# Convolution products as strips of the array: blocks 2 to 5 in four strips of 32 columns, blocks 6 to 8 in two of 64

## The reference

```
x = x + displaced(group_norm(x), offset)     # 48 groups of 8 channels
x = x + hadamard(group_norm(x))              # along the channels, 384 of 512
```

## Time and profile before

| | |
|---|---|
| time, median of 2 runs | 352.71 us |
| span of the profiled execution, first to last instruction | 361.2 us |
| PE / PEld busy | 162.4 us (45%) / 98.4 us (27%) |
| DVE busy | 246.9 us (68%) |
| ACT busy | 159.2 us (44%) |
| POOL busy | 124.9 us (35%) |
| convolution products L595, whole run | 306 matmuls, 41.3 us; 306 weight loads, 40.7 us |

### The profile page before, as it was taken

How to read it: one execution, slowest core, us unless ns; L and a number is a source line. 1 busy time by engine, 2 the same in 40 slices (tenths; PEclk the granted TensorE clock), 3 DMA queues, 4 the chain that set the end, 5 groups by cost and what they waited for, 6 DMA issues and landing times.

```text
span 361.2 us, 3084 instructions
## 1 busy us (share of the span) xinstructions
PE 162.4 (45%) x804; PEld 98.4 (27%) x804; DVE 246.9 (68%) x322; ACT 159.2 (44%) x205; POOL 124.9 (35%) x62
## 2 busy tenths in 40 slices
PE   0000004682796890300000008677676776767782
PEld 0000003682796790300000003222222222222230
DVE  1999999771874764100000047999999999899995
ACT  1029994940311200100000078787777777687720
POOL 0000000000521112000000007797979797979750
PEclk9999999995698996555555558698989889898898
DMA  6999999994388974373373300724996566874449
GB/s 227 414 410 409 409 370 355 406 249 102 71 216 216 279 210 122 53 87 44 44 87 44 44 0 17 292 100 186 356 373 248 191 147 198 311 294 181 190 181 360
DMA packets 21545, 76.67 MB, mean 212 GB/s; under 512 B 3824, under 2 KB 3952, under 8 KB 21376
## 3 DMA queue, kind: packets, MB, share of 16 engines
q1 hardware_dynamic: 18992, 69.62, 57.0%
q0 software_dynamic: 1616, 4.78, 4.8%
q10 hardware_dynamic: 912, 2.02, 4.7%
HBM read 46.42 MB, written 29.99 MB: 212 GB/s over the span
## 4 chain that ended last, share of the span: by engine, by line
DMA 25%; DVE 18%; issue 18%; another core or an unknown queue 16%; SPq 9%; ACTq 5%; ACT 5%; PE 2%; DVEq 0%; POOLq 0%
DMA ring<-x_pad 19%; DVE ring L917 9%; DVE parts L260 6%; SPq L267 5%; ACTq L267 5%; ACT blk L513 3%; DMA ring<-x_rows 2%; DMA blk<-x_pad 2%; DMA stat_rows<-blk_stat 2%; ACT parts L546 1%; SPq L271 1%; PE ps L656 1%; DVE blk_half L845 1%; PE ps L573 1%
## 5 line engine op out<-in xcount | busy, mean ns | idle before, releaser
L656 PE MATMUL ps<-parts,had_sb 128*128 128x512 f16 x384 | 101.6, 426 | 101.9 <-DVE parts L260 98.3
L513 ACT ACTIVATE blk<-ring,gn 128x1024 f32<-128x1024 f32 x48 | 58.6, 1230 | 85.4 <-DMA ring<-x_rows 59.9
L656 PEld LDWEIGHTS ps<-parts,had_sb 128*128 128x128 f16 x384 | 39.5, 107 | 163.7 <-DVE parts L260 105.2
L260 DVE TENSOR_TENSOR parts<-blk,parts 128x1024 f16<-128x1024 f32 x33 | 64.1, 1948 | 2.5 <-ACT parts L546 2.5
L917 DVE SCALAR_TENSOR_TENSOR ring<-ps,ring 128x1024 f32<-128x1024 f32 x48 | 57.2, 1210 | 0.0
L249 POOL TENSOR_TENSOR other_a<-blk 128x1024 f32<-128x1024 f32 x8 | 24.2, 3025 | 90.8 <-ACT parts L546 73.4
L253 POOL TENSOR_TENSOR blk<-blk 128x1024 f32<-128x1024 f32 x15 | 48.4, 3224 | 1.2
L582 PE MATMUL ps<-geo_sb,blk 128*128 128x128 f32 x72 | 13.6, 357 | 69.6 <-DMA blk<-x_pad 56.3
L595 PE MATMUL ps<-parts 128*128 128x64 f32 (+4 forms) x306 | 41.3, 301 | 7.3 <-ACT parts L475 6.2
L546 ACT ACTIVATE parts<-blk 128x1024 f16<-128x1024 f32 x40 | 41.2, 1048 | 4.2 <-POOL blk L253 2.8
L595 PEld LDWEIGHTS ps<-parts 128*128 128x128 f32 x306 | 40.7, 216 | 8.1 <-ACT parts L475 6.6
(11 more groups left out here) (105 smaller groups left out, 116.0 us busy)
## 6 DMA issues: line engine op xcount, KB each, us to landing
ring<-x_pad SPq DMA_DIRECT2D x20, 1536.0 KB, 15.3
out<-ring SPq DMA_DIRECT2D x13, 1536.0 KB, 6.3
blk<-x_pad SPq DMA_DIRECT2D x18, 512.0 KB, 8.3
x_rows<-blk POOLq DMA_DIRECT2D x9, 512.0 KB, 4.3
out<-ring SPq DMA_DIRECT2D x9, 512.0 KB, 3.7
ring<-x_rows ACTq DMA_DIRECT2D x5, 384.0 KB
ring<-x_rows SPq DMA_DIRECT2D x4, 384.0 KB
ring<-x_rows SPq DMA_DIRECT2D x9, 128.0 KB
```

The lines of the kernel that those rows point to most:

```text
L260: eng.tensor_tensor(parts[:, n % 2, 1, s, :], source, parts[:, n % 2, 0, s, :], ALU.subtract).then_inc(low_done[s], 1)
L513: act.activation(target, ring[:, t, place_of(i), :], ACT.Identity, bias=gn[:, t, i % BATCH, 1:2], scale=gn[:, t, i % BATCH, 0:1]).then_inc ...
L656: last = pe.matmul(sums[:, h, :], had_sb[:, sign, :], parts[:, n % 2, part, s, 512 * h:512 * (h + 1)], start=(at == 0 and part == 0), stop ...
```

## The change

One table `STRIP` gives each fast block a width, 128, 32 or 64. Where the width is below 128, each of the 17 products of the block is issued once for every strip: the stationary operand is cut along its columns (the pictures), and the result along the partitions of PSUM. The moving operand is the same for every strip. Blocks 0 and 1 keep one product of 128 columns.

```diff
+STRIP = (128, 128, 32, 32, 32, 32, 64, 64, 64)
...
-            def convolve_block(sums, pixels, weights):
+            def convolve_block(sums, pixels, weights, strip=128):
...
-                                last = pe.matmul(sums[:, bank, 32 * (a - 16 * bank):32 * (b - 16 * bank)],
-                                                 pixels[:, j, :], weights[:, a - (4 * j - 1):b - (4 * j - 1), :],
-                                                 start=(j == 3 * bank), stop=(j == 3 * bank + 4 and b == hi))
+                                for c in range(0, 128, strip):
+                                    last = pe.matmul(sums[c:c + strip, bank, 32 * (a - 16 * bank):32 * (b - 16 * bank)],
+                                                     pixels[:, j, c:c + strip], weights[:, a - (4 * j - 1):b - (4 * j - 1), :],
+                                                     start=(j == 3 * bank), stop=(j == 3 * bank + 4 and b == hi))
...
-                convolve_block(ps[2 + k % 2], flip[:, k % 2], conv_w[:, k]).then_inc(convolved, 1)
+                convolve_block(ps[2 + k % 2], flip[:, k % 2], conv_w[:, k], STRIP[k]).then_inc(convolved, 1)
```

## The result

The changed kernel took 359.67 us (358.97 to 360.37, 2 runs) against 352.71 us: a ratio of 1.0198, interval 1.0108 to 1.0287. That is inside the predicted range, at the edge of "within 2%". The first thing the profiles say, however, is that TensorE did not cost it.

What follows compares the result with a forecast made beforehand. ACT's walk over the row table, then nine patch transfers, was taken to bound the kernel, not PE. 14.4 us added to PE less 11 us covered gave 3.4 us, so 352.7 became 356 us; range 351.5 to 374.

Steps and rivals of the forecast that it cites:

- The gate: Before the first patch transfer at 147.81 us: ACT's walk over the row table holds it, not PE's convolutions.
- A gain of 7 us has no place to come from: Faster case: PE would have to stand on the path, and does so nowhere before 147.81 us; chance 0.02.
- the 3 us by which the blocks were out early: POOL goes on at 144.78 us, 3.0 us before ACT's first patch transfer; counted as room for PE.
- The cover: PE's waiting around blocks 2 to 8 and the blocks' early finish absorb 11 us of added TensorE work.
- The price of a pair: A weight load with its matmul on PE: 57 ns for strips of 32 and of 64, against 115 at full width.
- my own first rival: PE, blocks 2 to 5: strips stream singly, 10.6 us a block; +19 us, 372 us; chance 0.28, including 64 to 90 ns.
- The sum: Whole kernel: 14.4 us added to PE less 11 us covered gives +3.4 us, from 352.7 to 356 us.
- The change of mode: PE between transposes and strips, 93 to 137 us: 12 tiling mode changes at 160 ns, 1.9 us more, sum 358 us.
- The distance from the first patch transfer to the first L513, 62.3 us, should stay: Patch stage, 147.81 to 210.09 us: nine transfers as if one after another, 6.9 us each; distance fixed.
- Strips one after another: Same as my own first rival: strips on PE don't overlap, 360 to 374 us, chance 0.28.
- full price: PE, blocks 2 to 8: a pair keeps 115 ns; +46 us, some 399 us; chance 0.20 together with half the clock.
- half the clock: PE, blocks 2 to 8: clock halves, 57 ns becomes 114; much the same as full price; chance 0.20 together.

Runs made afterwards that it cites:

- the kernel convolved twice: Kernel before with the products of blocks 2 to 8 issued twice at full width: 373.9 ± 0.9 us against 359.3 ± 1.0 for the kernel before.
- the kernel with strips twice: Changed kernel with the products of blocks 2 to 8 issued twice as strips: 370.5 ± 1.5 us against 358.0 ± 1.1 for the kernel before.

## Why the prediction was right or wrong

- **The gate: right in the main, with less to spare than I gave it.** In both profiles shown the first patch transfer follows ACT's walk and not PE: with weight loads shorter by 8 us the walk began no earlier (ACT's first patch at 149.1), and "A gain of 7 us has no place to come from" held. But the 3 us by which the blocks were out early belong to one execution. In the three profiles of the changed kernel POOL's `stat<-stat_rows` stands 1.3, 0.4 and 1.3 us ahead of ACT's first patch, and in the second profile of the kernel before 0.5 us behind it (150.79 and 150.26), just as in the kernel convolved twice (162.53 and 162.00), where the blocks are the gate. That the last chain goes through SP's walk in the changed kernel does not make SP the gate: its packets waited behind ACT's.
- **The cover: right.** 11 us predicted, 12 to 13 measured, at one amount of added work.
- **The price of a pair: the step that failed.** I took 57 ns for a strip of 32 and 57 for one of 64, between bounds of 29 and 115. Measured were 19 and 41, below the lower bounds of 29 and 57. That bound let each load shrink with its columns but still put the loads one after another. Four strips together take 2.58 / 34 = 76 ns, two 2.77 / 34 = 81, where one full pair took 115. The bound that fits is in my own first rival: 2944 streamed columns at 0.9 ns are 2.65 us, once for all strips and not once for each. The starts in the trace show it set by set: the four matmuls of a set start 6 to 7 ns apart, and the next set starts at the earliest 135 ns later with 160 moving columns, 109 with 128, 82 with 96, 55 with 64 and 28 with 32, about 0.85 ns a column. Two strips of 64 with 32 columns mostly take 58 ns, half of a full pair's 115: there the load is the longer one. Loads and products of different strips ran side by side, and streaming became the price. The Trainium skill (TensorE: Matmul & The Clock Gate, Part 3) had three strips at 2.38 times the speed; here four do the work of four singly streamed ones in the time of one (10.6 us by the rival, 2.58 measured). The trace agrees with the page, and I should have let it lower the price.
- **The sum:** +3.4 us was to come from 14.4 us of added TensorE work. TensorE work fell, by 8 us of weight loads, so none of it came from there, and PE's wait ahead of the convolution of block 5, which was to vanish, grew from 3 to 8 us. That the forecast of 356 us stands near the measured 359.67 is no merit of that term.
- **The change of mode: seen, and smaller than estimated.** Ahead of the first strip load after a transpose stands an idle 0.17 us in the rows above; before, transposes and convolution follow on PEld without one. Where nothing else waits, the first strip's matmul starts 202 ns after the last transpose's (111 in the kernel before), and the next transpose 177 ns after the last strip's (112 before): 0.16 us a block, some 0.8 us in all where 1.9 was estimated. The Trainium skill's rule of the drain (TensorEngine Tiling (Array Packing), Key Properties) agrees with that.
- **"The distance from the first patch transfer to the first L513, 62.3 us, should stay": wrong.** It was 57.0 in the changed kernel and 54.9 in a second execution of the kernel before. I read a spread quantity off a single execution. "One after another" fits the profile that I had, where the packets of the two queues never mix; it does not fit those where they do. A sign stood in the table of times: the span of the profile, 361.2 us, lay 8.5 us above the median of the runs.
- **The rivals.** Strips one after another, full price, half the clock: none happened; only the stretch with the hole, 4.07 us, is as long as before. The clock was 1.00 in five of the seven stretches, 0.80 in the first and 0.68 in block 5, after that wait of 8 us; there too the loads took less than before.

## What to carry to other kernels

Column strips with the same moving operand share its streaming: the price of a set is the larger of one strip's load and one streaming, so they help where full-width loads are the bound, and help the kernel only if that engine is on the chain. Count the instructions too: many short ones seem to run an engine dry when the DMA engines are full. And before a difference of 2% is explained, the same kernel should be timed and profiled again, above all where its span and its times disagree.

## What the runs showed of the hardware

- Instructions reach TensorE in packets of 16 KB on a DMA queue, 256 instructions each. Strips used up 128 pairs in 2.7 us and then stood up to 5.7 us; the matmuls stood 13.1 us in 7 waits in the kernel with strips twice.
- Four column strips with the same moving operand cost one streaming: 76 ns a set on the mean, where one full pair costs 115.
- A transfer into eight partitions does not spread over 16 engines, whatever its packets: 7.3 to 7.9 packets are in flight on the mean with 48 KB packets, 8.0 to 8.3 with 2 KB ones. With 2 KB packets the patch took 39 to 50 us, with 48 KB packets 52 to 63.
- The mean time of the same 49152-byte packet was 5.0 to 6.7 us from one execution to the next. Packets with at least two of the other queue's beside them took 4.8 us, the others 6.4. Why is not shown.
